# The last pair's two depthwise convolutions as four-tile products on TensorE, with a new order of all engines' work

## What is computed

```python
x = x + dwconv(x, cpe1_w, cpe1_b)
y = ln2d(x, norm1_w, norm1_b)
act_res = silu(conv1x1(y, act_proj_w, act_proj_b))
y = conv1x1(y, in_proj_w, in_proj_b)
t = silu(dwconv(y, dwc_w, dwc_b))                 # first depthwise convolution: "dwc"
q, k = elu(t @ qk_w + qk_b) + 1                   # split in two halves; v = t
z = 1 / (q . mean(k) + 1e-6)
attn = rope(q) @ (rope(k)^T v / n) * z
lepe = dwconv(t, lepe_w, lepe_b)                  # second depthwise convolution: "lepe"
y = conv1x1((attn + lepe) * act_res, out_proj_w, out_proj_b)
x = x + y
x = x + dwconv(x, cpe2_w, cpe2_b)
y = ln2d(x, norm2_w, norm2_b)
out = x + conv1x1(gelu(conv1x1(y, fc1_w, fc1_b)), fc2_w, fc2_b)
```

## Time and profile before

| | us |
|---|---|
| median of 3 runs | 760.77 |
| lowest, highest | 759.55, 765.72 |
| the profiled execution | 761.57 |
| its span, first to last instruction | 759.7 |
| TensorE busy | 723.6 (95%) |
| VectorE busy | 506.2 (67%) |
| ScalarE busy | 465.0 (61%) |
| GpSimd busy | 298.7 (39%) |
| mean granted TensorE clock | 0.984 of full |

### The profile page before, as it was taken

How to read it: one execution, slowest core, us unless ns; L and a number is a source line. 1 busy time by engine, 2 the same in 40 slices (tenths; PEclk the granted TensorE clock), 3 DMA queues, 4 the chain that set the end, 5 groups by cost and what they waited for, 6 DMA issues and landing times.

```text
span 759.7 us, 19754 instructions
## 1 busy us (share of the span) xinstructions
PE 723.6 (95%) x8464; PEld 462.0 (61%) x8464; DVE 506.2 (67%) x646; ACT 465.0 (61%) x657; POOL 298.7 (39%) x230
## 2 busy tenths in 40 slices
PE   4989999999999999999999999999999899899997
PEld 3867676765565555576654655666754454577654
DVE  6576424569994999967943542499997688956301
ACT  3665444795854967687576953795824577823244
POOL 6322203230699310869501231022699211496000
PEclk9999999999999999899999999999999989999999
DMA  2230000000100103000102200000000100011101
GB/s 46 48 75 2 17 17 17 1 2 2 32 17 2 33 16 64 17 18 2 33 16 56 54 19 17 2 3 1 17 17 16 33 17 2 16 33 21 29 17 32
DMA packets 50504, 16.76 MB, mean 22 GB/s; under 512 B 45584, under 2 KB 50320, under 8 KB 50418
## 3 DMA queue, kind: packets, MB, share of 16 engines
q1 hardware_dynamic: 49906, 15.46, 9.4%
q10 hardware_dynamic: 512, 0.04, 0.0%
HBM read 4.87 MB, written 3.54 MB: 11 GB/s over the span
## 4 chain that ended last, share of the span: by engine, by line
PE 63%; DVE 22%; POOL 7%; ACT 4%; issue 4%; DMA 0%; SPq 0%; DVEq 0%; ACTq 0%; POOLq 0%
PE ps L606 19%; PE ps L596 7%; DVE QS L1203 7%; PE ps L853 7%; DVE CT L1213 6%; PE ps L697 6%; PE ps L672 4%; PE ps L683 3%; PE ps L843 3%; PE ps L781 2%; PE ps L651 2%; PE ps L660 2%; POOL KX L1323 1%; PE ps L724 1%; POOL KX L1316 1%
## 5 line engine op out<-in xcount | busy, mean ns | idle before, releaser
L1349 POOL TENSOR_TENSOR SC<-SC,mx 128x768 f32<-128x768 f32 x48 | 75.5, 1575 | 191.3 <-DVE mx L1156 191.3
L606 PE MATMUL ps<-XP,wdw 48*64 48x384 f32 x1728 | 144.5, 483 | 1.2 <-POOL XP L1354 0.6
L1213 DVE SCALAR_TENSOR_TENSOR CT<-TP,vec_sb,CT 112x768 f32<-112x768 f32 x96 | 127.8, 1353 | 1.1
L606 PEld LDWEIGHTS ps<-XP,wdw 48*64 48x64 f32 x1728 | 70.1, 132 | 68.5 <-issue 54.8
L1203 DVE SCALAR_TENSOR_TENSOR QS<-XP,vec_sb,QS 112x768 f32<-112x768 f32 x96 | 100.6, 1092 | 1.1 <-ACT QS L1004 0.7
L1152 DVE TENSOR_TENSOR SC<-ps,bias_sb 128x768 f32<-128x768 f32 x48 | 45.8, 954 | 60.4 <-PE ps L672 60.1
L606 PE MATMUL ps<-G,w_sb 48*64 48x384 f32 x864 | 72.5, 484 | 0.0
L697 PEld LDWEIGHTS ps<-vx,PT 128*128 128x128 f32 x576 | 66.3, 192 | 7.8 <-issue 5.0
L697 PE MATMUL ps<-vx,PT 128*128 128x52 f32 x576 | 68.4, 274 | 0.3 <-ACT PT L938 0.3
L853 PEld LDWEIGHTS ps<-ident_sb 128*128 128x128 f32 x484 | 58.5, 199 | 12.8 <-issue 11.6
L853 PE MATMUL ps<-ident_sb 128*128 128x128 f32 x484 | 63.1, 287 | 0.0
(11 more groups left out here) (166 smaller groups left out, 1263.9 us busy)
## 6 DMA issues: line engine op xcount, KB each, us to landing
XP<-in_x_dram SPq DMA_DIRECT2D x48, 72.0 KB, 2.4
YB<-YF SPq DMA_DIRECT2D x48, 72.0 KB, 2.2
XP<-XB SPq DMA_DIRECT2D x48, 72.0 KB, 2.4
out_dram<-XB SPq DMA_DIRECT2D x24, 144.0 KB, 2.3
rope_th_sb<-in_rope_th_dram SPq DMA_DIRECT2D x1, 441.0 KB
w_sb<-in_w_dram SPq DMA_DIRECT2D x2, 81.0 KB
wfc_sb<-in_wfc_dram SPq DMA_DIRECT2D x4, 36.0 KB
wln_sb<-in_const_dram SPq DMA_DIRECT2D x6, 9.0 KB
```

The lines of the kernel that those rows point to most:

```text
L606: mm = pe.matmul(slot(job)[half(c, HALF), r * BANK:r * BANK + SPX], w[half(r), tap * HALF:(tap + 1) * HALF], shifted(t, d * CROWS + c * WI ...
L1213: dve.scalar_tensor_tensor(out=ct, in0=win, scalar=v(f"lepe_{TAPS[k]}"), in1=ct, op0=ALU.mult, op1=ALU.add).then_inc(lepe_step, 1)
L1349: pool.tensor_tensor(sc, sc, bc_last(mx[:, (u % NSC) * 12:(u % NSC) * 12 + 12], TOK), ALU.subtract).then_inc(sub_ready, 1)
```

## The change

Only the last pair (pair 3) is computed in another way; for the others the jobs are the same in another order.

- **dwc:** c10 and c11 to c18 of pair 3 are gone. In their place: dw (PE, conv with diagonal weights over XP into PSUM, 72 instructions), dc (ACT, copy to T0), dt (PE, turned with the identity eye2_sb, 8 instructions, which takes back the swap of halves), and ts reads dt's PSUM and adds the bias.
- **lepe:** c20 and c21 to c28 of pair 3 are gone. In their place: le (PE, conv over TP), lc (ACT, copy to CT), lt (PE, identity), and am reads lt's PSUM, adds the bias and the attention in one instruction. le needs t of the chunk and of its neighbours, dw the in-projection of the same.
- **Weights:** two VectorE jobs, wl (over w2_sb, after the last cv) and wd (over wdw0, after the last d0), each one multiply of 112x576.
- **Places:** q of pair 3 lies in G's memory (free after the last cv), so qe waits for cv.3.2 and no longer for f2.2.2. The third chunk's CT lies in the other XP (free after d3.2.2). ge.3 waits for f2.2.2 and no longer for am.3.2.
- **Engines:** qc and ym of pair 3 go from GpSimd to VectorE. GpSimd keeps kr and qs.
- **Orders:** all five tables are new, in pairs 0 to 2 too. Filler is 100 units in place of 242: 12 in the first strips, 26 from va.1.1 to d3.0.1 (2, 5, 1, 4, 14), and 62 from f2.2.1 on: 2 and 5 ahead of f2.2.1 and f2.2.2, 14 ahead of d3.3.0, 13 ahead of va2.3.2, 16, 6 and 6 ahead of the three last f2. There is none ahead of at.3.0 to at.3.2.

```diff
--- before.py
+++ after.py
@@ PE_ORDER, from the last norm of pair 3 on @@
-    kk.3.0@1+5 dn.3.0@3 dn.3.1@2 dn.3.2@0 at.3.0@1+29 at.3.1@3+7 at.3.2@1+9 op.3.0@2+2 op.3.1@3+4 d3.3.0@0+31
-    op.3.2@1 xc2.3.0@2+2 va2.3.0@3+4 f12.3.0@0+14 f11.3.0@1 f10.3.0@2 d3.3.1@3 f2.3.0@0 xc2.3.1@2 d3.3.2@1
-    va2.3.1@3 xc2.3.2@0+2 va2.3.2@2+13 f12.3.1@1 f11.3.1@3 f10.3.1@0 f2.3.1@2+16 f11.3.2@3 f12.3.2@0 f10.3.2@1
-    f2.3.2@2+6
...
+    dn.2.0@3 va.3.1@0 dn.2.1@1 va.3.2@2 kk.2.0@3 at.2.0@3 at.2.1@0 ip.3.1@2 ac.2.2@3 ip.3.2@1 dn.2.2@2 dw.3.0@0
+    op.2.0@3 op.2.1@1 dt.3.0@2 at.2.2@0 dw.3.1@3 d3.2.0@1 op.2.2@2 vt.3.0@0 kt.3.0@3 dt.3.1@1 xc2.2.0@2 dw.3.2@0
+    le.3.0@2 va2.2.0@3 dt.3.2@1 kv.3.0@0 vt.3.1@2 kt.3.1@0 f11.2.0@3 le.3.1@1 le.3.2@2 kv.3.1@0 f12.2.0@3
+    vt.3.2@1 f10.2.0@0 kt.3.2@3 f2.2.0@1 d3.2.1@0 d3.2.2@1 kv.3.2@3 xc2.2.1@0 xc2.2.2@2 kp.3.0@1 va2.2.1@3
+    q.3.0@0 kk.3.0@2 va2.2.2@1 q.3.1@2 q.3.2@3 f12.2.1@0 f11.2.1@1 f10.2.1@2 ac.3.0@3 dn.3.0@1 ac.3.1@2 dn.3.1@3
+    at.3.0@2 ac.3.2@1 dn.3.2@2 at.3.1@3 at.3.2@1 lt.3.0@3 lt.3.1@2 lt.3.2@3 f2.2.1@1+2 f12.2.2@0 op.3.0@2
+    op.3.1@3 f11.2.2@0 f10.2.2@1 f2.2.2@2+5 op.3.2@3 d3.3.0@0+14 d3.3.1@1 xc2.3.0@2 d3.3.2@3 xc2.3.1@0 va2.3.0@1
+    xc2.3.2@2 va2.3.1@3 va2.3.2@0+13 f12.3.0@1 f11.3.0@2 f10.3.0@3 f2.3.0@0+16 f12.3.1@3 f11.3.1@2 f10.3.1@1
+    f2.3.1@0+6 f12.3.2@3 f11.3.2@2 f10.3.2@1 f2.3.2@0+6
...
@@ ACT_ORDER, the same stretch @@
+    rs.3.1 rs.3.2 z.2.1 ie.3.1 ar.2.2 ie.3.2 z.2.2 dc.3.0 c20.2.2 ts.3.0 dc.3.1 x4.2.0 ve.3.0 ke.3.0 sq2.2.0
+    ts.3.1 dc.3.2 lc.3.0 rs2.2.0 ts.3.2 ke.3.1 ve.3.1 ge1.2.0 lc.3.1 ge2.2.0 ve.3.2 ge0.2.0 ke.3.2 x4.2.1 lc.3.2
+    x4.2.2 sq2.2.1 sq2.2.2 rs2.2.1 qe.3.0 rs2.2.2 qe.3.1 qe.3.2 ge1.2.1 ge0.2.1 ar.3.0 ar.3.1 z.3.0 z.3.1 ar.3.2
+    z.3.2 ge2.2.1 ge2.2.2 ge1.2.2 ge0.2.2 x4.3.0 x4.3.1 sq2.3.0 x4.3.2 sq2.3.1 rs2.3.0 sq2.3.2 rs2.3.1 rs2.3.2
...
@@ DVE_ORDER, the same stretch @@
+    kk.3.0 yn2.2.1 qo.3.0 yn2.2.2 qo.3.1 qo.3.2 qc.3.0 qc.3.1 az.3.0 qc.3.2 az.3.1 am.3.0 az.3.2 am.3.1 am.3.2
+    ym.3.0 ym.3.1 o.2.1 oz.3.0 oz.3.1 ym.3.2 o.2.2 oz.3.2 yn2.3.0 yn2.3.1 yn2.3.2 o.3.0 o.3.1 o.3.2
...
+        def q_of(i):
+            return Gp[:, :, :].rearrange("p y x -> p (y x)") if i == PAIRS - 1 else Q
...
+        def ct(i, n):
+            if (i, n) == (PAIRS - 1, CH - 1):
+                return XP[PAIRS % 2][0:RG].rearrange("p y x -> p (y x)")[:, 0:CPX]
+            return CT[(i * CH + n) % 2]
...
+        def diagonals(dve, w, name):
+            taps = vec_sb[:, VI[f"{name}0"]:VI[f"{name}0"] + 9]
+            return dve.tensor_tensor(w[:, :].rearrange("p (t c) -> p t c", c=HALF), bc_mid(eye2_sb[0:RG, :], 9),
+                                     bc_last(taps, HALF), ALU.mult)
...
+                elif name == "dw":
+                    for d in around(n):
+                        wait_read(pe, ("ip", i, d))
+                    pe.wait_ge(dwc_weights, 1)
+                    conv(job, wdw0, XP[i % 2], n)
+                elif name == "dt":
+                    wait_read(pe, ("dw", i, n))
+                    turned(job, eye2_sb, T0[n])
+                elif name == "le":
+                    for d in around(n):
+                        wait_t(pe, i, d)
+                    pe.wait_ge(lepe_weights, 1)
+                    conv(job, w2_sb, TP, n)
+                elif name == "lt":
+                    wait_read(pe, ("le", i, n))
+                    turned(job, eye2_sb, ct(i, n))
...
+                elif name == "dc":
+                    job = ("dw", i, n)
+                    wait_filled(act, job)
+                    wait_filled(act, ("at", i - 1, n))
+                    act.activation(pairs(T0[n]), two(job), ACT.Copy).then_inc(free(job), 2)
+                elif name == "ts" and i == PAIRS - 1:
+                    job = ("dt", i, n)
+                    wait_filled(act, job)
+                    act.wait_ge(lepe_step, LEPE_STEP[8, i - 1, halo_last(n)])
+                    act.activation(inner8(TP, n), two8(job), ACT.Silu, bias=v("dwc_b")).then_inc(free(job), 2)
...
-                    if i:
+                    if i == PAIRS - 1:
+                        wait_filled(act, ("cv", i, CH - 1))
+                    elif i:
                         wait_filled(act, ("f2", i - 1, CH - 1))
...
+                elif name == "am" and i == PAIRS - 1:
+                    job = ("lt", i, n)
+                    wait_read(dve, ("at", i, n))
+                    wait_filled(dve, job)
+                    dve.scalar_tensor_tensor(out=pairs(ct(i, n)), in0=two(job), scalar=v("lepe_b"),
+                                             in1=pairs(chunk(q_of(i), n)), op0=ALU.add, op1=ALU.add)\
+                       .then_inc(free(job), 2)
...
+                elif name == "qc":
+                    wait_read(dve, ("q", i, n))
+                    wait_filled(dve, ("ac", i, n))
+                    dst = chunk(LV[i % 2], n)
+                    ty, tx = rope_of(n, 0)
+                    dve.tensor_tensor(eight(dst), eight(chunk(q_of(i), n)), ty, ALU.mult).then_inc(qc_half, 1)
+                    dve.wait_ge(qc_half, n + 1)
+                    dve.tensor_tensor(rows16(dst), rows16(dst), tx, ALU.mult).then_inc(qc_last, 1)
```

## The result

The changed kernel takes **794.11 us** (three runs: 787.50, 797.01, 794.11) against 760.77 us. The ratio is **1.041, 95% interval 1.037 to 1.045**: slower by 4%, 36 us above the forecast of 758 and outside its range. The profiled execution was the fastest of the three, 787.50 us, with a span of 785.5 us. The steps of the forecast went to a span of 757.9, so 27.6 us of span are to be explained; all that follows is made in spans. (The other two executions were granted a clock of 0.967 and 0.969 instead of 0.980 and took 10 and 7 us more; that part of the 36 is not taken apart here.)

The account below looks back on a forecast made before the run. TensorE was taken to bound the kernel (660.5 of 759.7 us work, 99.2 waiting), the tail being a chain of latencies. Steps (a) to (d), 4.3 us behind and -1.5 at the start gave span 757.9, forecast 758, range 748 to 768.

Parts of the forecast that it names:

- The six convolutions and identity products: Last pair, added to TensorE: six convolutions 35.4 us, six identity products 4.6, together 40 us of work.
- qc 3.3 us a chunk: Last pair's qc on VectorE: two tensor_tensor at 1.6 us, 3.3 us per chunk, bounds 2 to 5.
- ScalarE's copies at 0.90: Last pair's dc and lc: 0.90 us each, replacing c10 and c20 one for one, so nothing added.
- table load 1.28: ScalarE: each table load costs 1.28 us and the next ACTIVATE follows at once; five loads in (c).
- (a): Start to the end of pair 2's windows: same work, smaller fills from 252 to 300 us, -4 to -5, taken as -5 us.
- the head's -1.5: First 60 us: TensorE's 6.8 us of half clock may be lost or not, -3.4 or 0, taken as -1.5 us.
- (b): To the end of d3.2.2: +45.4 us of jobs ahead of it, -14 of waits filled; ends at 671.3.
- (c): From d3.2.2 to d3.3.0: ScalarE sets the pace, move back to XP takes 5 us; d3.3.0 at 712.
- the slower rival: New tail: half clock in two 6.83 us stretches, with qc at its upper bound, +12 to 770 us; chance 0.14.
- (d): From d3.3.0 to the last f2: 43.1 us instead of 49.0, since op.3.2 and fills no longer stand between.
- 50 us off VectorE: Last pair's taps removed from VectorE, some 50 us: shrunk to nothing in (c), as TensorE arrives 26 us later at d3.2.2.
- The faster one: Between pairs 0 and 1: waits and half clock vanish too, 10 us more gained, 748 us; chance 0.28.

Follow-up runs that it names:

- e1: Changed kernel with the job orders of the kernel before up to w1.3.5 (some 550 us), its own orders behind: 781.63 us, ratio 1.024.
- e9: Whole change, orders of the kernel before kept up to about 540 us, moved job by job behind, filler sized anew: 770.31 us, ratio 1.010.
- e2: Kernel before, computation unchanged, with the changed kernel's orders up to about 530 us and its old orders behind: 790.60 us, ratio 1.035.
- e10: Kernel before with only the last pair's qc on VectorE, orders kept up to 560 us and moved behind, filler sized anew: 749.73 us, ratio 0.982.
- e11: As e10, with the last chunk's lepe convolution of the last pair also on TensorE: 748.94 us, ratio 0.981.

## Why the prediction was wrong

- **The six convolutions and identity products, +40 us of work: right.** L647 gave 35.2 for the convolutions; the identity products (L637 on eye_sb) 5.2. The rest of the +44.1 fits half clock.
- **qc 3.3 us a chunk, ScalarE's copies at 0.90, table load 1.28: right.** 10.0 us for three qc; the copies (L1088) took 0.81.
- **(a), -5 us to the end of pair 2's windows, and the head's -1.5: wrong, 16.6 of the 27.6 us.** The step read the fewer units of fill as fewer waits, and said "VectorE is full here before and after with the same work", without following the new order on any engine from its first job. What TensorE spent other than on work up to f2.0.2 was 53.8 us, where 43.7 stood before and 37 were forecast: 5 us were lost by 100 us, in the first strips, and the rest from 250 on, behind taps that begin 4.5 us later and beside more table loads. e1 and e9 give it back with the old order (44.9 and 42.6), e2 brings it about without the change. The sign named for (a), f2.0.2 before 320, looked only to the fast side; it ended at 340.9.
- **From there to kk.2.0: 3.7 us more**, a stretch that the walk took as unchanged.
- **(b), to d3.2.2, +45.4 of work and -14 of waits: right to 0.9 us.** From kk.2.0 to d3.2.2 the time that was not work rose by 2.3 instead of 14.7 before.
- **(c), to d3.3.0 in 40.7 us: 46.4 measured, mis-sized by 5.7.** ScalarE set it as described, but from x4.2.2 (691.85) to the end of z.3.2 (720.53) it took 28.7 us instead of 26.9, with 4.1 us of pauses, 3.4 of them for TensorE and VectorE. From there to the end of oz.3.1 (730.2) it was 9.7 instead of 8, with TensorE's identity products at half clock until 722. And the move back to XP took 7.2 instead of 5: the issues of two chunks' DMAs alone hold SP for 5.50 us.

```profile
729.31 5.50 SPq L546 DMA_DIRECT2D XP<-XB  x8
```

  The sign that was named for the slower rival came (granted clock 0.69 in 700 to 720), and so did its place, with a chance of 0.14; the rest of its 12 us did not.
- **(d), 43.1 us to the last f2: right** (43.8).
- **That 50 us off VectorE come to nothing in the tail: not contradicted.** The whole change on the old head costs 7.1 us of span, though with qc's move in it, which alone gained 8.2. The forecast's own sum without (a) and the head comes to 764.4, near e9's 766.8; e9's tail is another order than the one walked, so that is partly luck.
- The rivals: none came to 785. The faster one (waits in pairs 0 and 1 vanish) sat on the stretch that decided, with the wrong sign; its mirror, that the new order of those pairs is worse, was missing, though the diff rewrites all five orders nearly line by line.

Of the signs that were named, the 432 instructions came; TensorE's busy time was 732.3 instead of 727, VectorE's 465.8 instead of 450 to 460.

The five add up: 16.6 + 3.7 + 0.9 + 5.7 + 0.7 = 27.6 us. What stays open is which jobs of the head's order do it. The first strips, the late cv.0.0 and d0.0.2, VectorE's late first tap and ScalarE's added table loads are what the traces show; none was moved alone, so this part of the cause is argued, and only that it lies in the head's order is shown.

## What to carry to other kernels

A change that comes with a new order of everything is two changes, and the order is the larger risk: walk it from the first job, on every engine that is nearly full there, before costing the part that the diff is named after. Filler hides who is waited for: taken out of this kernel, the trace said that it was GpSimd. Compare two executions from the point where their orders part, since the part they share can differ by 5 us. And move work where the receiving engine waits on the very thing that is moved: three lepe convolutions took back 15 to 18 us of waiting for 15 to 20 of work, three dwc ones 0 to 4 for 19 to 23.

## What the runs showed of the hardware

- In these kernels the clock was worth less than its busy time says. In the changed kernel more filler took 12.6 us off TensorE's work and 2.0 us off the span of the profiled execution. Without any filler the kernel before had 27.7 us more of work (688.2 against 660.5) and 11.1 us more of span.
- Half clock lasts: behind a bare wait of 6.32 us the 72 instructions of a d3 took 8.88 us instead of 6.04; in the changed kernel, behind waits of 1.68 and 1.14 us, groups of eight instructions took 1.53 us instead of 0.85 until 721 us.
- Whether it comes is not fixed by the order: e10 and e11 have the same orders and the same filler up to f2.0.2, and ended it at 330.8 and 325.8 us. The first was granted 0.93 in 300 to 350, the second 1.00.
- A VectorE tensor_tensor of 112 x 768 took 0.95 us alone and 2.11 to 2.56 beside GpSimd's rope products, and those took 2.19 and 2.41 instead of 1.47 and 1.81. The Trainium skill (SBUF, State Buffer, section on who interferes with whom) says that a VectorE instruction with two SBUF inputs contends with a GpSimd one that reads SBUF; the traces agree, and add that here both sides paid.
